# Residual sum in tiles, a longer trail of the gelus and a last store in two pieces, in a transformer block with top-k masking

## What is computed

```python
x = x + topk_mask(side, cond, x, 5120)          # called xm below
ada = cond @ ada_w + ada_b                      # shift1, scale1, gate1, shift2, scale2, gate2
x1 = ln(xm) * (1 + scale1) + shift1
att = attention(x1 @ qkv_w + qkv_b)             # 16 heads of 128
y = xm + gate1 * (att @ out_w + out_b)          # called x2 in the kernel
h = gelu((ln(y) * (1 + scale2) + shift2) @ ffn_w1 + ffn_b1)
y = y + gate2 * (h @ ffn_w2 + ffn_b2)
out = xm + y
```

## Time and profile before

| | us |
|---|---|
| median of three runs | 1692.68 |
| lowest, highest | 1692.13, 1695.88 |
| the profiled execution, its own time | 1692.08 |
| its span, first to last instruction | 1690.1 |
| PE busy | 1621.2 (96%) |
| DVE busy | 1160.2 (69%) |
| ACT busy | 858.1 (51%) |
| POOL busy | 157.5 (9%) |

### The profile page before, as it was taken

How to read it: one execution, slowest core, us unless ns; L and a number is a source line. 1 busy time by engine, 2 the same in 40 slices (tenths; PEclk the granted TensorE clock), 3 DMA queues, 4 the chain that set the end, 5 groups by cost and what they waited for, 6 DMA issues and landing times.

```text
span 1690.1 us, 22637 instructions
## 1 busy us (share of the span) xinstructions
PE 1621.2 (96%) x8317; PEld 1357.5 (80%) x8317; DVE 1160.2 (69%) x2556; ACT 858.1 (51%) x1623; POOL 157.5 (9%) x93
## 2 busy tenths in 40 slices
PE   2879999999999999999999999999999999999998
PEld 2868888888788888888778888888878888888887
DVE  7867877767776877776774887776775666665421
ACT  4546666655835455552743555554571545544240
POOL 4612221214040000000000000000000000000000
PEclk9999999999999999999999999999999999999999
DMA  9913444447565223224446133134354331332453
GB/s 343 336 59 115 169 136 155 159 144 255 187 249 215 115 76 125 100 100 150 156 193 241 64 125 125 50 125 150 150 193 181 125 125 54 129 117 93 157 199 124
DMA packets 63853, 256.32 MB, mean 152 GB/s; under 512 B 4352, under 2 KB 4480, under 8 KB 60800
## 3 DMA queue, kind: packets, MB, share of 16 engines
q1 hardware_dynamic: 63456, 254.56, 40.7%
q10 hardware_dynamic: 288, 0.33, 0.1%
HBM read 200.34 MB, written 54.53 MB: 151 GB/s over the span
## 4 chain that ended last, share of the span: by engine, by line
PE 89%; DVE 6%; ACT 3%; issue 1%; DVEq 1%; DMA 0%; SPq 0%
PE bank L1153 25%; PE bank L1155 24%; PE bank L1154 24%; PE bank L1252 7%; PE bank L1415 2%; DVE tb L829 1%; PE bank L1278 1%; PE bank L1320 1%; PE bank L1315 1%; PE bank L1316 1%; DVE prob L1006 1%; PE bank L1200 1%; PE bank L1182 1%; ACT prob L704 1%; PE bank L1204 1%
## 5 line engine op out<-in xcount | busy, mean ns | idle before, releaser
L1153 PE MATMUL bank<-xT,w 128*128 128x512 f32 x704 | 279.9, 398 | 0.5 <-POOL w L538 0.5
L704 ACT ACTIVATE prob<-bank,nbias 128x512 f32<-128x512 f32 x256 | 176.6, 690 | 201.9 <-DVE nbias L1003 201.9
L1155 PE MATMUL bank<-xT,w 128*128 128x512 f32 x704 | 274.5, 390 | 0.0
L1154 PE MATMUL bank<-xT,w 128*128 128x512 f32 x704 | 274.2, 390 | 0.0
L1153 PE MATMUL bank<-act,w 128*128 128x512 f32 (+1 forms) x576 | 217.6, 378 | 0.8 <-DVE act L967 0.8
L1155 PE MATMUL bank<-act,w 128*128 128x512 f32 (+1 forms) x576 | 211.1, 367 | 0.0
L1154 PE MATMUL bank<-act,w 128*128 128x512 f32 (+1 forms) x576 | 210.8, 366 | 0.0
L1014 DVE TENSOR_TENSOR probT<-bank,probT 128x512 fp32r<-128x512 f32 x256 | 158.6, 682 | 24.7 <-ACT probT L714 24.6
L997 DVE TENSOR_REDUCE rowmax<-bank 128x1 f32<-128x512 f32 x256 | 174.8, 683 | 0.0
L1155 PEld LDWEIGHTS bank<-xT,w 128*128 128x128 f32 x704 | 132.1, 188 | 27.9
L1153 PEld LDWEIGHTS bank<-xT,w 128*128 128x128 f32 x704 | 132.1, 188 | 26.1 <-POOL w L538 0.9
(11 more groups left out here) (151 smaller groups left out, 3065.4 us busy)
## 6 DMA issues: line engine op xcount, KB each, us to landing
w<-split_weights SPq DMA_DIRECT2D x152, 1024.0 KB, 5.3
split_weights<-w SPq DMA_DIRECT2D x40, 1024.0 KB, 6.1
wraw<-weights_in SPq DMA_DIRECT2D x48, 512.0 KB, 4.2
adaw<-ada_w_in SPq DMA_DIRECT2D x4, 1536.0 KB, 13.3
split_weights<-xT SPq DMA_DIRECT2D x6, 1024.0 KB, 7.6
xr<-x_in SPq DMA_DIRECT2D x4, 1024.0 KB, 5.7
out<-x SPq DMA_DIRECT2D x4, 1024.0 KB, 4.4
adj<-x_in SPq DMA_DIRECT2D x3, 1024.0 KB, 7.0
```

The costliest lines, as they stand in the source:

```text
L704: nc.scalar.activation(prob[:, i, :], bank[i][:, :], ACT.Exp, bias=nbias[:, i:i + 1], scale=SCALE, accum_out=rowsum[:, i:i + 1]).then_inc( ...
L1153: pe.matmul(dst, w_hi_ap, x_hi_ap, start=first, stop=False)
L1154: pe.matmul(dst, w_hi_ap, x_lo_ap, start=False, stop=False)
L1155: return pe.matmul(dst, w_lo_ap, x_hi_ap, start=False, stop=last)
```

## The change

- In sequences 1 to 3 (not 0) ACT's gelus trail: in the loop it issues the count of slot n and then the gelus of tile n - 2. The last two rounds of the loop take the counts of (mlp_out,0,0) and (0,1) with the gelus of tiles 14 and 15. DVE's low parts trail by three: the step of slot n, then the low part of tile n - 3; its last three rounds take the steps of (mlp_out,0,0) to (0,2), each ahead of the low parts of tiles 13, 14 and 15.
- In all sequences the single addition of `xm` to `x2` ahead of the loop is replaced by four additions of one row tile each: two behind the step of (mlp_out,0,3), two behind the gate of unit 0 at (mlp_out,1,0); each pair ends with a drain.
- The last sequence's store is made in two pieces: columns 0 to 383 after the sum of unit 2, columns 384 to 511 after the last sum.

```diff
+def gelu_lag(b):
+    return (0, 1) if is_first(b) else (2, 3)
+
+def mlp_place(n):
+    return ("mlp_in", n // 4, n % 4) if n < KC else ("mlp_out", 0, n - KC)
...
+            def store_last(signal, columns):
+                wait_apart(sp, signal, B)
+                sp.dma_start(out[B - 1].rearrange("(p i) d -> p i d", p=P)[:, :, columns], x2[:, :, columns])\
+                    .then_inc(out_stored, 16)
...
-            store(B - 1)
-            sp.wait_ge(out_stored, 16 * B + STORE_CREDIT)
+            store_last(y2_added, slice(0, D - P))
+            store_last(out_ready, slice(D - P, D))
+            sp.wait_ge(out_stored, 16 * (B + 1) + STORE_CREDIT)
...
# ACT
-                for f in range(KC):
-                    next_count(("mlp_in", f // 4, f % 4))
+                lag = gelu_lag(b)[0]
+                for n in range(KC + lag):
+                    next_count(mlp_place(n))
+                    f = n - lag
+                    if f < 0:
+                        continue
...
-                        next_count(("mlp_out", u, r))
+                        if 4 * u + r >= lag:
+                            next_count(("mlp_out", u, r))
...
# DVE
+                def add_masked(i):
+                    V.tensor_tensor(x2[:, i, :], x2[:, i, :], xm[:, i, :], ALU.add)
...
-                V.tensor_tensor(x2[:, :, :].rearrange("p i d -> p (i d)"),
-                                x2[:, :, :].rearrange("p i d -> p (i d)"),
-                                xm[:, :, :].rearrange("p i d -> p (i d)"), ALU.add)
-                for f in range(KC):
-                    step_at(("mlp_in", f // 4, f % 4))
-                    if f:
-                        hidden_lo(b, f - 1)
-                hidden_lo(b, KC - 1)
+                lag = gelu_lag(b)[1]
+                for n in range(KC + lag):
+                    if n < KC or lag > 1:
+                        step_at(mlp_place(n))
+                    if n >= lag:
+                        hidden_lo(b, n - lag)
                 for u in range(4):
                     for r in range(4):
                         if u and r == 0:
                             mlp_gate(u - 1)
-                        step_at(("mlp_out", u, r))
+                        if 4 * u + r >= lag or lag == 1:
+                            step_at(("mlp_out", u, r))
+                        if (u, r) in ((0, 3), (1, 0)):
+                            add_masked(2 * u)
+                            add_masked(2 * u + 1)
+                            dve.drain()
```

## The result

| | before | after |
|---|---|---|
| median of the runs taken together (22 each), us | 1693.55 | 1696.10 |
| lowest, highest | 1691.91, 1697.13 | 1694.11, 1698.79 |
| the profiled execution, its own time | 1692.08 | 1697.53 |
| its span | 1690.1 | 1695.6 |
| PE, DVE, ACT, POOL busy | 1621.2, 1160.2, 858.1, 157.5 | 1623.5, 1165.0, 856.7, 157.9 |

The ratio of after to before is 1.0014 (95% interval 1.0007 to 1.0020): about 2.4 us slower, which is within the 0.2% that was called the same. The forecast was +2.2 us.

What follows compares the result with a forecast made beforehand. PE, busy 1621.2 of 1690.1 us, bounds the kernel, so only its waits count. Terms -0.3 + 4.7 + 1.7 - 3.9 + 1.3 - 1.3 = +2.2 us give a median of 1694.9; 8-in-10 range 1689.0 to 1697.0.

Steps and rivals of the forecast that it cites:

- First slots of sequences 1 and 2: PE's wait for the two counts there goes, as DVE and ACT finish in time: -1.94 us in each sequence.
- Step 15: Sequences 1 and 2: PE newly waits for the low part of tile 15, +0.65 us each, bounds nothing and 0.9.
- First slot of the first sequence: With the addition ahead of the loop gone, split and low parts come sooner: -0.3 us, bounds 0 and -1.0.
- The stall at (mlp_out,3,1): First sequence: four sum pieces and POOL's splits delay DVE's chain, so PE waits for the gates: +4.7 us.
- The clock: TensorE's clock falls to half in the first sequence's gap of 4.35 us: +1.7 us, bounds 0 and 3.8.
- The last store: End of the run: last piece lands 2.6 us after issue instead of 3.9: -1.3 us, bounds -2.0 and +0.5.
- The sum: Whole kernel: all terms together make +2.2 us, a profiled time of 1694.3 us and a median of 1694.9.
- A: Rival: as the forecast, but TensorE's clock stays up in the first sequence's gap; 1693.2 us, chance 0.27.
- B: Rival: POOL costs DVE's chain no more than before, stall 2.0 us, no clock fall; -2.2, 1690.5 us, chance 0.10.
- C: Rival: no stall at (mlp_out,3,1) in the first sequence, gates ready in time; -4.2, 1688.5 us, chance 0.12.
- D: Rival: TensorE's clock, once down at (mlp_out,3,1), stays down for longer; 1697.0 us with 3.8 us, chance 0.09.
- E: Rival: ACT's count at the first slot still comes late, the 1.94 us stall stays twice; 1698.8 us, chance 0.04.

## Why the prediction was right, step by step

- **First slots of sequences 1 and 2**, -1.94 each: -1.89 each. Right, with its cause, as the trail alone shows: DVE and ACT had low parts and gelus ahead of the step, and with them gone the count is ready in time.
- **Step 15**, +0.65 each: +0.67 and +1.01, with the longer trail alone +0.66 and +0.68. Right in mechanism. The 1.01 has a gap of 0.43 us between two DVE instructions at (mlp_out,0,2) that no engine ended. Five other traces with the pieces in all sequences have it at the same place, those of the longer trail alone and of the first sequence's sum ahead don't:

```profile
1264.68 0.21 DVE L917 TENSOR_SCALAR cand<-cand,step_up 128x1 f32<-128x1 f32 x1 [0.43 <-issue]
```

The last two have it elsewhere or not at all, and the kernel before has one of the same kind and size one step later, where PE doesn't wait for DVE; what makes it was not found:

```profile
1261.84 2.35 DVE L909 TENSOR_SCALAR_CACHE_REDUCE eqm<-low,cand 128x2048 bf16<-128x2048 f32 x1 [0.46 <-issue]
```

So 0.35 us of the second step 15 is not the wait that was forecast. The bound of 0.9 was a little too narrow for it.
- **First slot of the first sequence**, -0.3: -0.30.
- **The stall at (mlp_out,3,1)**, +4.7: +3.85 to the transposes and 0.3 for the second unit, 4.2 in all. The terms held: four pieces 2.6; the third split, taken at 2.3, measured 2.04 by its removal. That splits and chain take exclusive turns is shown by cutting them. What was placed wrongly is who is held by the first: the small copy, not the scan. From the comparison on, the chain ran 0.3 to 0.5 us ahead of the one worked out (its end at 490.03 against 490.35, both counted in after's trace), and the gates with it.
- **The clock**, +1.7: +1.1, by the 1.14 us between the kernels with the gap full and empty. It fell, as forecast, and came back 3.0 us after PE had started again. The term was mis-sized: 3.0 us at half speed are 1.5 us of work, and 0.3 of them lay under the wait for the second gate. The 17 warming matmuls gave 1.9 since the slow stretch there is longer: the first eight distances are 0.43 us or more, the ninth 0.36, and only then 0.23. The windows there print a clock of 1.00, so that it was at half is read from the distances alone. And the four transposes taken to lie in that time were all eight, with three matmuls. The 2.6 us of the end of the run, from which the fall was forecast, is one value of many: in the 14 traces the clock falls 1.0 to 4.1 us behind the last matmul, in five of them later than 3.7 us. That it fell in this gap was likely and not certain.
- **The last store**, -1.3 with 2.6 us to landing: 2.6 us, -1.3 in the trace, -1.05 between the medians alone.
- **The sum.** The stall and the clock were each taken 0.5 to 0.6 us too high; step 15 gave 0.4 us and the first slots 0.1 us of that back. The terms as measured make +1.7 us and not +2.2. What lies between them and the measured +2.4 are differences in code that is the same (+0.5 in these two traces) and a second stretch at half clock that some executions may have. So the mechanisms and the places of the forecast are right, and that the sum came within 0.2 us is in part luck. The median itself, 1696.10, is 1.2 us over the forecast's 1694.9: 0.9 of that is the kernel before, 1693.55 over 22 runs and not the 1692.68 of three.

Of the rivals, A (the clock stays up) falls by the windows. B (POOL costs no more than before) falls by the third split cut: 2.0 us. C (no stall) falls by the first line of waits; the time that it gave, 1688.5, is what the kernel with the first sequence's sum ahead reaches (1688.7), since that one has no such stall. D (the clock down for long at that place) is not in the trace. A milder form may be in others: 11 of the 22 executions of after have a mean clock of 0.997 or 0.998, and their median is 0.8 us over that of the other 11 (1696.7 against 1695.8). E falls by the slots.

**Left open.** In which stall the clock fell in the six executions with a mean of 0.997 or 0.998 was not seen; two traces show it behind a stall of 1.7 us at a first slot, and the other 12 stalls of that length show none. Nor was it settled why 315.9 us and at other times 316.6 lie between the transposes of `z` and the next first slot.

## What to carry to other kernels

An edit that is free on average can cost in the one pass of a loop that has other company: here the sums are hidden by 4.4 us of slack in sequences 1 and 2, by the absence of a chain in the last, and by nothing in the first, where GpSimd still splits weights; keep the old order for that pass alone. When VectorE and GpSimd take turns, moving VectorE's chain by 2.6 us can add a whole GpSimd instruction to it, so work out the turns again after the shift instead of adding the shift alone. And a short stall of TensorE can have a second price in its clock. Removing it paid here each time; filling it with matmuls gave 1.1 us at the gap of 3.7 us, perhaps 1.5 us at one pair of short stalls, and nothing in the two other kernels.

## What was not expected of the hardware

- A VectorE copy of 8 elements a row took 2.21 us beside a GpSimd instruction with two inputs, and 0.17 us without it.
- TensorE's granted clock fell from 1.00 to 0.50 in two traces behind a stall of only 1.73 us, for 3.4 us and at a cost of 1.6 us, while 12 other stalls of 1.7 us left it up. In the kernel with the third split cut, seven matmuls in each such stall left all 11 executions at a mean clock of 1.000, where six of eleven had 0.997 or 0.998.
- In the gap of 3.7 us it fell 3.3 us after the last matmul's end. At the ends of the 14 traces that time is anything from 1.0 to 4.1 us.
- A VectorE scan of 2048 elements a row held a GpSimd instruction of 32 columns for 4.0 us.
